# A causal attention stage inside a four-stage kernel: the mask moves from TensorE into VectorE's maximum, and each maxima unit gets a score unit beside it

## What is computed

```python
x = x + attn_a(layernorm(x), Wk, Wq, Wv, Wo, bo, kln_w, kln_b, qln_w, qln_b)
x = x + ffn(layernorm(x), ...)          # 8 experts, top 2
x = x + attn_b(layernorm(x), ...)       # 16 channels, sigmoid of all pairs
x = x + ffn(layernorm(x), ...)
```

```python
k, q, v = ((x @ W).reshape(b, t, 16, 8) for W in (Wk, Wq, Wv))
k, q = layernorm8(k, kln_w, kln_b), layernorm8(q, qln_w, qln_b)
dot = einsum('bqhs,bkhs->bhqk', q, k) * 8 ** -0.5
dot = where(tril(ones((t, t))), dot, -inf)
out = einsum('bhqk,bkhs->bqhs', softmax(dot), v).reshape(b, t, 128) @ Wo + bo
```

## Time and profile before

| what | value |
|---|---|
| median of 3 runs | 2841.32 us (2831.55 to 2841.84) |
| span of the profiled execution, first to last instruction | 2834.4 us |
| attention stage in it | about 40 to 735 us |
| busy in the whole span | PE 93%, DVE 63%, ACT 56%, POOL 29% |
| granted TensorE clock, mean | 0.969 of 2.4 GHz |

### The profile page before, as it was taken

One profiled execution on the slowest core, in us unless ns is written; L12 is line 12 of the kernel. 1 busy time (PEld: TensorE's weight loads), 2 busy tenths in 40 slices (PEclk: granted clock), 3 DMA queues, 4 the chain that ended last, 5 costly groups with the idle time before them and its releaser, 6 DMA issues. The chain is left out here.

```text
span 2834.4 us, 54508 instructions
## 1 busy us (share of the span) xinstructions
PE 2635.7 (93%) x19182; PEld 1713.2 (60%) x19182; DVE 1789.9 (63%) x3491; ACT 1578.4 (56%) x2843; POOL 820.0 (29%) x1181
## 2 busy tenths in 40 slices
PE   5999998998689979999999999999999999996997
PEld 3555565655478845666555665555555555554886
DVE  7777777786466745555665556555556655555666
ACT  2666666666454455555555556555566555554443
POOL 4142422525345311111111111112121123322642
PEclk8999999999799979999999999999999999997998
DMA  6500000001424258888878888887888788885222
GB/s 109 82 16 16 8 16 16 16 9 31 119 83 157 94 130 196 195 196 196 204 184 200 196 196 189 190 187 177 188 189 190 183 201 200 206 199 203 71 87 85
DMA packets 190430, 383.21 MB, mean 135 GB/s; under 512 B 45281, under 2 KB 100714, under 8 KB 188810
## 3 DMA queue, kind: packets, MB, share of 16 engines
q1 hardware_dynamic: 181578, 362.55, 53.9%
q0 software_dynamic: 8640, 17.84, 1.8%
HBM read 38.10 MB, written 39.86 MB: 28 GB/s over the span
## 5 line engine op out<-in xcount | busy, mean ns | idle before, releaser
L3050 DVE STREAM_TRANSPOSE m_turned<-m_sig 128x1024 f32<-128x1024 f32 x512 | 613.6, 1227 | 429.5 <-ACT m_sig L2820 201.1
L2643 PE MATMUL m_v_ps<-m_sig,m_tok 128*64 128x512 f32 x2048 | 468.2, 599 | 0.0
L2656 PE MATMUL m_v_ps<-m_sigT,m_tok 128*64 128x256 f32 x4064 | 461.5, 380 | 3.2 <-DMA m_sigT<-m_turned 3.2
L1208 DVE TENSOR_REDUCE a_maxima<-a_bank 128x1 f32<-128x512 f32 (+4 forms) x624 | 367.4, 643 | 121.1 <-PE a_bank L707 73.2
L2627 PE MATMUL m_f_ps<-m_swap,m_own 64*128 64x512 f32 x1536 | 426.2, 404 | 15.6 <-DMA m_swap<-m_own 7.4
L894 ACT ACTIVATE a_prob<-a_bank 128x512 f32<-128x512 f32 (+1 forms) x608 | 322.2, 586 | 201.0 <-PE a_bank L719 197.5
L2627 PE MATMUL m_f_ps<-m_own,m_swap 64*128 64x512 f32 x1536 | 426.4, 404 | 0.0
L2656 PEld LDWEIGHTS m_v_ps<-m_sigT,m_tok 128*64 128x64 f32 x4064 | 289.4, 137 | 200.3 <-issue 54.8
L2916 POOL TENSOR_TENSOR m_own<-m_uv,m_own 128x1024 fp32r<-128x1024 f32 x64 | 152.0, 2375 | 813.4 <-ACT m_own L2782 813.4
L2820 ACT ACTIVATE m_sig<-m_f_ps 128x1024 f32<-128x1024 f32 x256 | 248.3, 1022 | 245.4 <-issue 147.5
L2627 PEld LDWEIGHTS m_f_ps<-m_swap,m_own 64*128 64x128 f32 x1536 | 271.6, 186 | 99.9 <-ACT m_sig L2806 25.8
(11 more groups left out here) (509 smaller groups left out, 4268.6 us busy)
## 6 DMA issues: line engine op xcount, KB each, us to landing
m_sigT<-m_turned SPq DMA_DIRECT2D x2042, 128.0 KB, 2.3
m_swap<-m_own SPq DMA_DIRECT2D x64, 256.0 KB, 3.2
f_t_rows<-f_sent_rows SPq DMA_DIRECT2D x142, 65.0 KB, 2.1
f_sent_rows<-a_proj SPq DMA_DIRECT2D x34, 260.0 KB, 9.5
k_apart<-a_kT SPq DMA_DIRECT2D x64, 128.0 KB, 2.4
m_swap<-m_own SPq DMA_DIRECT2D x64, 128.0 KB, 3.2
f_h<-back_rows SPq DMA_DIRECT2D x8, 512.0 KB, 5.6
rows<-back_rows SPq DMA_DIRECT2D x6, 512.0 KB, 4.9
```

The lines of the kernel that those rows point to most:

```text
L1208: dve.tensor_reduce(maxima[:, qt, h:h + heads, part], src, AX.X, ALU.max).then_inc(u.free(), 1)
L2643: mm = pe.matmul(v2_ps[h * RANK:(h + 1) * RANK, :], tok[p][:, 0, j + s * SIDE, :], sig[j % 2][s][:, h * HALF:(h + 1) * HALF], start=(j == ...
L2656: mm = pe.matmul(v1_ps[h * RANK:(h + 1) * RANK, g * 2 * P:(g + 1) * 2 * P], tok[p][:, 1, jj, :], sigT[g][:, :, 2 * h:2 * h + 2, jj, :].rea ...
L3050: dve.transpose(turned[g][:, :, q, :, :], sig[j % 2][s][:, :].rearrange("p (t j a) -> p j t a", j=4, a=STACK)).then_inc(turn_ready, 1)
```

## The change

1. The mask matmul (L707) and `ident16` go. `mask` becomes 512 wide, zero but for its last 128 columns. For a piece of a maxima unit that holds the diagonal, VectorE runs `tensor_tensor_reduce` (add the mask, write the sum to the new scratch tile `masked_out`, accumulate the maximum into `maxima`) in place of `tensor_reduce`. Pieces off the diagonal keep `tensor_reduce`, into `first_max`.
2. Units are cut anew: 40 maxima and 40 score units, each for a single head; narrow pieces of two tiles share a bank. In a group the maxima work is 48 pieces, 32 masked and 16 not.
3. Maxima units lie beside score units 0 to 37 (6 to 37 in the first group) in place of 9 to 36.
4. For that, keys and queries are turned two groups ahead (at score units 24, 31, 33 and 35), and the spread goes in two halves of four DMAs each: low keys after score unit 28, high keys at the start of the next group. `kT` is one tile, not two.
5. ScalarE, not VectorE, empties the turned queries and the second half of `qmT`.
6. `PLACE` goes; its steps are written as score units. `a_prob` is laid out anew (`PROB_AT`), and `weigh` moves (`WEIGHED_AFTER`).

```diff
-    SCORE_UNITS, MAX_UNITS = 38, 39
+    SCORE_UNITS, MAX_UNITS = 40, 40
...
-            begin, end, made = PLACE[4], 36, 0
+            begin, end, made = 6 if first else 0, 37, 0
...
+        MAX_PIECES = (((0, 0, P), (1, 0, 2 * P)), ((2, 0, 3 * P),), ((3, 0, HALF),), ((4, 0, HALF),), ((5, 0, HALF),),
+                      ((4, HALF, 5 * P), (5, HALF, 6 * P)), ((6, 0, HALF),), ((6, HALF, 7 * P),), ((7, 0, HALF),), ((7, HALF, SEQ),))
+        MAXES = [(pieces, (h + GROUP // 2) % GROUP) for pieces in MAX_PIECES for h in range(GROUP)]
...
-                if masked:
-                    mask = k["mask"][:, :].unsqueeze(1).broadcast_to([P, heads, P])
-                    mm = pe.matmul(out[:, :, k1 - k0 - P:k1 - k0], k["ident16"][:, :], mask, start=False, stop=True)
...
-                dve.tensor_reduce(maxima[:, qt, h:h + heads, part], src, AX.X, ALU.max).then_inc(u.free(), 1)
+                masks = any(k1 == (qt + 1) * P for qt, _, k1 in pieces)
+                if masks:
+                    masked_by.append(u.n)
+                    if len(masked_by) > MASKED_OUTS:
+                        u.wait_emptied(dve, masked_by[-1 - MASKED_OUTS])
+                for qt, k0, k1 in pieces:
+                    width = k1 - k0
+                    scores = src[:, col:col + width]
+                    masked = masked_out[(len(masked_by) - 1) % MASKED_OUTS][:, col:col + width]
+                    col += width
+                    if k1 < (qt + 1) * P:
+                        ins = dve.tensor_reduce(first_max[:, qt % HALF_T, h:h + 1], scores, AX.X, ALU.max)
+                        continue
+                    ins = dve.tensor_tensor_reduce(out=masked, in0=scores, in1=k["mask"][:, HALF - width:HALF], scale=1.0,
+                                                   scalar=MASKED, op0=ALU.add, op1=ALU.max, accum_out=maxima[:, qt, h:h + 1])
+                ins.then_inc(u.free(), 1)
...
+                if two_ahead and i in (24, 31, 33, 35):
+                    yield ("keys", "queries")[i // 33], (24, 31, 33, 35).index(i) % HALVES_OF
+                if two_ahead and i == LOW_KEYS_DONE + 1:
+                    yield "spread_low", 0
...
+                    elif what == "queries":
+                        empty(u, half_of(qT[g % 2], n))
+                    elif what == "turn_high":
+                        empty(u, half_of(qmT[g % 2], 1))
```

More of the change, by code:

```diff
@@ L371, in attention_phase @@
         steps = sb("a_steps", [P, TILES])
-        k_apart = [k["k_apart0"], k["k_apart1"]]
+        k_apart = [k[f"k_apart{i}"] for i in range(2)]
         ones_column = k["ones"][:, 0:1]
@@ L490, in sequence @@
         def sequence(g, prev, prep, follows, stage=None):
-            keys_ahead = prep or g < HALVES_OF
-            begin, end, made = PLACE[4], 36, 0
-            if prev and follows:
-                yield "spread", 0
+            two_ahead, first = prep or g < HALVES_OF, follows and not prev
+            begin, end, made = 6 if first else 0, 37, 0
             for i in range(SCORE_UNITS):
                 yield "score", i
+                if prev and follows and i == 0:
+                    yield "spread_high", 0
                 if g == 1 and i == 0:
@@ L554, in sequence @@
+                if prev and g == 0 and 32 <= i <= 36:
+                    yield ("add_x", 0) if i == 32 else ("out_stats", i - 33)
+                if follows and i == 21:
+                    yield "turn_low", 0
                 if stage is not None:
@@ L645, in _ @@
             u = Units(0, 0)
             u.n += 3 + TILES + 2
-            spread(u, 0, u.n)
+            for half in range(HALVES_OF):
+                u.wait_emptied(sp, u.n - 1 + half)
+                spread(0, half)
             clear_sent("f1")
             u.n += 2 + MAX_UNITS + 2
-            keys = group(u, 0, False, False, True)
+            high = group(u, 0, 0, False, False, True)
             clear_sent("f2")
@@ L712, in turn_shifted, with scores @@
                 return turn_tiles(u, heads_of(q_st, g), tiles_of(n))
-            def scores(u, g, n, shifted=()):
-                j, h, heads, q0, q1 = SCORES[n]
-                out = by_head(u.next(), q1 - q0, heads)
+            def scores(u, G, n, shifted=()):
+                pieces, h = SCORES[n]
+                out, col = u.next(), 0
                 u.wait_empty(pe, *shifted)
-                for i in range(heads):
-                    mm = pe.matmul(out[:, i, :], k_apart[g % 2][:, h + i, j * P:(j + 1) * P], qmT[g % 2][:, q0:q1], start=True, stop=True)
+                for j, q0, q1 in pieces:
+                    mm = pe.matmul(out[:, col:col + q1 - q0], k_apart[G % 2][:, h, j * P:(j + 1) * P], qmT[G % 2][:, q0:q1], start=True, stop=True)
+                    col += q1 - q0
                 mm.then_inc(unit_full, 1)
@@ L890, in weights @@
             def weights(u, n):
-                j, h, heads, q0, q1 = SCORES[n]
-                src = by_head(u.next(), q1 - q0, heads)
+                pieces, h = SCORES[n]
+                src, width = u.next(), sum(q1 - q0 for _, q0, q1 in pieces)
+                to, off = prob_of(*pieces[0][0:2])
+                start = pieces[0][1] - off
                 u.wait_full(act)
-                act.activation(prob[j % 2][:, h:h + heads, prob_cols(j, q0, q1)], src, ACT.Exp).then_inc(u.free(), 1)
+                act.activation(to[:, h, start:start + width], src[:, 0:width], ACT.Exp).then_inc(u.free(), 1)
             def empty_out(G):
@@ L1411, in group @@
                         out_stats(b - 1, n)
-                    elif what in ("score", "keys", "turn_low", "turn_tokens", "turn_z", "project"):
+                    elif what in ("score", "keys", "queries", "turn_low", "turn_high", "turn_tokens", "turn_z", "project"):
                         u.next()
```

309 lines of the change are left out of this document (149 added, 160 removed).

## The result

The changed kernel takes 2810.28 us (median of 4 runs, 2807.82 to 2812.77), the kernel before 2838.15 us (2831.55 to 2841.84) beside it: ratio 0.9904 [0.9888, 0.9921], 28 us less. 2796 was forecast. The time lies in the range and the sign is right; of the forecast 45 us, 28 came.

What follows compares the result with a forecast made beforehand. No engine was taken as full: VectorE and TensorE take turns through six banks. Terms summed to -5.6 + 32r, -3.4 us a period (41.5 to 38.1); -44.7 us in all from 2841.3 gave 2796, range 2752 to 2858.

Steps and rivals of the forecast that it cites:

- The head is filled: Score units at a group's start without maxima beside them: filling them removes 3.8 us of VectorE idle time a period.
- a stretch of batch work on VectorE stalls the ring as before: In the rival "nothing much moves" (chance 0.07): batch work stalls the six-bank ring, head idle time returns elsewhere, 2841 us.
- The mask leaves TensorE: Maxima units: a mask matmul costs 0.13 us, 23 make 3.0 us a period, of which 1.0 is saved.
- Casts leave VectorE: Three 128x512 casts go from VectorE to ScalarE: VectorE saves 1.8 us a period, ScalarE's added time is covered.
- The second instruction: Each of 32 masked pieces brings a VectorE instruction writing 128x1: plus 2.2 us a period at 0.07 us each.
- r: Time of one 128x1 instruction after a masked pass: bounded by 0.02 and 0.23 us, taken as 0.07.
- more pieces: VectorE's maxima: 48 pieces in place of 39 at equal columns, 0.08 us fixed cost each, plus 0.7 us a period.
- add-and-reduce: Masked passes on VectorE: add-and-reduce costs 0.01 us more than a reduction, 32 times, plus 0.3 us a period.
- The opening, +3.2, and the first period: Group 0's maxima, VectorE alone, grow by 3.2 us; the first period regains only part of its head, +2.5.
- The turn at r = 0.157: Value of r where the forecast gain becomes a loss; rival that the second instruction waits for the pass: chance 0.20.
- the half rate: Rival, chance 0.05: VectorE's masked pass runs at half rate, +166 us, 2962 us.
- TensorE was the bound among the maxima: Rival, chance 0.08: all 3.0 us of the masks come back each period, 30 us more gain, about 2765 us.

Runs made afterwards that it cites:

- e11: Changed kernel plus a VectorE maximum over 32 columns of the bank ahead of each masked unit, 24 a period: 2826.1 us.
- e7: Changed kernel plus one bf16 matmul on TensorE, adding zeros, for each of the 24 masked units of a group: 2830.8 us.
- e3: Changed kernel with the maxima beside score units 9 to 37 in every group, so the head has none: 2822.9 us.
- e9: Changed kernel with maxima starting after the ninth score unit only in g = 1 groups that prepare a batch: 2804.5 us.
- e2: Kernel before, old order, with only the mask moved to VectorE's masked pass, 48 passes a group: 2823.4 us.
- e1: Changed kernel with the mask added by a bf16 matmul on TensorE again and plain maxima on VectorE: 2827.2 us.
- e4: Changed kernel with the three casts (both halves of qT, second half of qmT) back on VectorE: 2810.8 us.
- e5: Changed kernel with VectorE's work for the next batch split into short pieces among the maxima: 2811.1 us.
- e8: Changed kernel plus a VectorE copy of the 128x128 mask within SBUF ahead of each masked unit: 2851.7 us.
- e13: Changed kernel with ScalarE copying variances instead of taking square roots, so no other function table is loaded in batch-preparing groups: 2811.7 us.
- e14: e9 with ScalarE copying variances in place of the square roots: 2805.0 us.

## Why the prediction was right in sign and too large in size

*Where the idle time is.* "So no engine is full; VectorE is idle for 10.0 us of a period" was read rightly, but the step that followed was not: the sum took each microsecond of VectorE's work and idle time at its full length. e11 measured 0.45 for VectorE, e7 0.75 for TensorE. In the plain period the bound is close to TensorE's, in the first part of a g = 1 group VectorE's.

*The head is filled, -3.8 a period, -57 in all.* This is the step that failed: "I take the 3.8 us of idle time in it as gone". e3 measured 13 us, under 0.9 a period: 3.4 in g = 0, 1.3 in the plain period, a loss of 1.8 in g = 1 where a batch is prepared. The missing input that I looked for was not the trouble; TensorE's wait for `k_apart` was one of 2.6 us. The row that the 3.8 came from already spoke against it: in the same four heads TensorE was busy for 22.08 of 23.8 us. In the plain period TensorE is busy 32.91 of 33.24 us, so a maximum made in the head mostly moves work of the engine that is full. In g = 1 the head had VectorE's batch work in it, and none of the four heads of the earlier trace rows is that of a g = 1 group. "a stretch of batch work on VectorE stalls the ring as before" stood in the text, in a rival with 0.07, and is what e9 and the windows show for the g = 1 periods.

*The mask leaves TensorE, -1.0 a period.* Right in size: e2 gives 11.7 / 15 = 0.8 (with the more passes in it), e1 18.1 / 15 = 1.2. It is the largest single part of the gain that came. The two numbers behind it were off in opposite ways: a mask was priced at 0.13 us of TensorE and in e7 one takes 0.08 in the plain period (1.89 / 24), a third of it was to reach the end and 0.75 does. That they gave about the right term is in part luck.

*Casts leave VectorE, -1.8 a period.* Mis-sized; e4 puts all three back and measures 1.0 us in 15 periods, under 0.1 a period. ScalarE's busy time was forecast well (27.6 us a period, forecast 28.0), its cost to the period taken as nothing without a run of its own.

*The second instruction, r = 0.07.* Mis-sized; at most 0.01 by the start distances. By the prediction's formula r = 0.01 gives -80.5 + 5 = -75 us, and the forecast would have been 2766, 44 us below what was measured: that 2796 came out near is partly luck, since the error of r hid a part of the others. In the sum, r was 31 us too dear, the heads 44 us and the casts 27 us too good; 45 + 31 - 44 - 27 leaves a gain of 5 us, and 28 were measured. The 23 us between are not assigned by a run of their own. The sum's "more pieces" and "add-and-reduce" stand in it with 15 us (1.0 a period at full length, which at e11's share would be 7, an estimate), so some 8 may lie there, and 3 are the mask; each run also takes one part out of the finished kernel, and such parts need not add.

*The opening, +3.2, and the first period.* The opening ended at 66.8 us as before (66.9). Its second half, which has no gap in either trace, did grow: from 15.69 us to 16.2 (50.55 to 66.77), 0.5 us for 5 more passes and 16 accumulator reads. That fits the 0.08 us for a piece, and not the 0.07 for a read. The first half got 0.7 us back: it goes from 42.5 to 50.6 us where it went to 51.3, since before VectorE had waited 0.24 us for a mask matmul and an instruction of `shift` is 0.4 us shorter. The first period became 0.4 us shorter, where the sum has 0.9.

*What would show it.* Period 38: no, 40.1. VectorE 86%: no, 77% (30.78 of 40.1). No gap of maxima at a group's start: true, and in g = 1 TensorE has one of 3.26 us there (2.9 before). A masked 512 lasts 0.68 us, not over 0.8, and TensorE waited nowhere for one of ScalarE's casts of `qT` or `qmT` (only weight loads did, for at most 0.3 us). The turn at r = 0.157 and the half rate did not come; "TensorE was the bound among the maxima" is half true, in the plain periods.

What stays open: why g = 2 gained nothing. By e3 its filled head is worth 0.9 us, and by e1 (42.3 us) the mask's move 1.8, yet e2, the old order with the mask moved, is slower there than the kernel before (41.9 against 40.2). The granted clock in these periods is 0.87, 0.92 and 0.92 where it was 0.96 in all three; e4 took 38.8 us twice at 0.96 and 40.1 us at 0.91. Whether the lower clock is a cause or follows from TensorE's waits is not shown, and I tried neither an empty head there alone nor another place for the squares (e5 only halved their sums). In g = 1, 1.9 of the 2.6 us between the changed kernel and e9 remain in e5 at the same mean clock as in e9; how much of the rest is the clock is not shown either.

## What to carry to other kernels

Before counting an engine's idle time as a reserve, price it: add a small instruction of a known length to each unit on one engine at a time and read which share comes through (here 0.45 and 0.75). A mean period hides stages with different bounds; cut it where the busiest engine changes, and fill idle time only in the part where the engine that gets the work is not the full one. The shares hold for the place where the instruction was put: the same engine's time came through with 0.45 in front of each masked unit, and with next to nothing when three casts went back to it and ScalarE lost them. A step that evens out a schedule can still be wrong in the one group where the other work is front-loaded, and leaving that group out (one condition, e9) was worth a fifth of the whole change.

## What the runs showed of the hardware

- The read of an accumulator is a row of 83 ns, but starts with the next pass and adds at most about 0.01 us to the distance between passes (0.61 us for masked passes of 512 columns, 0.60 for plain ones).
- A maximum with an added mask, PSUM and SBUF in, 128x512 out to SBUF, takes what the plain maximum of the same width takes: 683 against 684 ns.
- A bf16 copy within SBUF on VectorE waited for a running GpSimd pass, up to 1.96 us for an instruction of 0.13 (e8), while passes that read PSUM and one SBUF tile kept their 0.28 and 0.41 us beside the same GpSimd pass. The Trainium skill ("SBUF — State Buffer", section "SBUF: two separate sides") has an exclusive pair of ports for GpSimd and for VectorE's operations in a two-port mode, where the later one waits for the whole instruction; this trace agrees, with the copy's end at 359.21 and GpSimd's at 359.16.
- Two loads of a function table of 1.28 us each in a group cost nothing that these runs can tell, with a filled head (e13: 2811.7 us without them, 2810.3 with) and with an empty one (e14: 2805.0, 2804.5 with).
